# A decoder layer on one core: attention's queries, keys and values computed from high and low parts, their weights loaded a stage earlier

## The reference

```python
x = layernorm(x + mixer(x))        # layernorm, k, v, r = 256x256 projections, decayed cumulative sum, Wo
x = layernorm(x + xattn(x, ctx))   # this stage is changed
x = layernorm(x + ffn(x))          # dense expert + 32 routed experts, 4 per token, capacity 1280

def xattn(x, ctx):                 # 8 heads of 64
    q = x @ Wq                     # 256 -> 512
    k, v = ctx @ Wk, ctx @ Wv      # 192 -> 512
    attn = softmax(q k^T / 8)      # per batch and head, 128 x 128
    return (attn v) @ Wout + bout  # 512 -> 256
```

## Time and profile before

| what | us |
|---|---|
| median of three runs | 2421.14 |
| profiled execution | 2423.74 |
| its span, first to last instruction | 2422.2 |
| setup and mixer, about | 0 to 275 |
| attention with routing, about | 275 to 1131 |
| experts, about | 1140 to 2010 |
| combine, about | 2010 to 2422 |

### The profile page before, as it was taken

How to read it: one execution, slowest core, us unless ns; L and a number is a source line. 1 busy time by engine, 2 the same in 40 slices (tenths; PEclk the granted TensorE clock), 3 DMA queues, 4 the chain that set the end, 5 groups by cost and what they waited for, 6 DMA issues and landing times. The chain is left out here.

```text
span 2422.2 us, 51520 instructions
## 1 busy us (share of the span) xinstructions
PE 2123.5 (88%) x13848; PEld 1722.7 (71%) x13848; DVE 1574.4 (65%) x3953; ACT 1211.0 (50%) x3430; POOL 1351.9 (56%) x1648
## 2 busy tenths in 40 slices
PE   6999699999999999830999999999999956878884
PEld 3555356666666666530999999999999955777774
DVE  4666335667667666632777777777777743766666
ACT  2555245444455445410777777777777742222221
POOL 3666303456655655555555555555555535777775
PEclk9999899999999999955999999999999987989897
DMA  4000112322411321301666666666667643444343
GB/s 127 33 0 0 46 50 78 98 62 59 117 59 59 107 69 59 101 13 58 209 236 239 237 234 228 237 242 228 238 227 243 238 143 126 132 121 136 119 137 91
DMA packets 240146, 317.12 MB, mean 131 GB/s; under 512 B 38073, under 2 KB 161761, under 8 KB 240098
## 3 DMA queue, kind: packets, MB, share of 16 engines
q1 hardware_dynamic: 210594, 258.19, 31.9%
q0 software_dynamic: 29504, 58.37, 8.2%
HBM read 233.34 MB, written 83.14 MB: 131 GB/s over the span
## 5 line engine op out<-in xcount | busy, mean ns | idle before, releaser
L969 POOL DMA_INDIRECT slot_token<-tok,a_slot_i x256 | 267.9, 1047 | 231.0 <-issue 95.6
L1354 POOL DMA_INDIRECT e_xg<-x_rows,e_tok x188 | 197.4, 1050 | 346.2 <-DMA e_tok<-slot_token 188.1
L1639 POOL DMA_INDIRECT f_row<-expert_rows,f_idx x256 | 273.9, 1070 | 89.9 <-issue 76.7
L1532 DVE TENSOR_TENSOR e_hid<-e_sg,e_u 128x256 f32<-128x256 f32 x368 | 155.1, 421 | 133.3 <-PE e_u L1207 106.7
L1482 ACT ACTIVATE e_sg<-e_g 128x256 f32<-128x256 f32 x368 | 141.2, 384 | 179.6 <-PE e_g L1207 179.6
L852 ACT ACTIVATE a_prob<-a_s,a_ntop 128x128 f32<-128x128 f32 x512 | 180.2, 394 | 0.8 <-DVE a_ntop L1149 0.5
L1730 ACT ACTIVATE f_sg<-f_g 128x512 f32<-128x512 f32 x64 | 38.2, 597 | 222.1 <-PE f_g L1207 222.1
L1363 POOL TENSOR_TENSOR e_wd1l<-e_raw_d,e_wd1h 128x256 fp32r<-128x256 f32 x184 | 130.4, 742 | 30.0 <-ACT e_wd1h L1461 29.8
L1207 PE MATMUL f_d<-f_wdh,f_hth 128*128 128x256 f32 x256 | 85.6, 334 | 63.6 <-DVE f_htl L1759 63.6
L1363 POOL TENSOR_TENSOR e_wd0l<-e_raw_d,e_wd0h 128x256 fp32r<-128x256 f32 x184 | 130.9, 743 | 7.3 <-ACT e_wd0h L1461 6.4
L1207 PE MATMUL e_d<-e_wd1h,e_ht1h 128*128 128x256 f32 x368 | 108.3, 294 | 24.5 <-issue 24.5
(11 more groups left out here) (262 smaller groups left out, 7522.9 us busy)
## 6 DMA issues: line engine op xcount, KB each, us to landing
e_raw_g<-in_eg SPq DMA_DIRECT2D x94, 512.0 KB
e_raw_u<-in_eu SPq DMA_DIRECT2D x94, 512.0 KB, 4.2
e_raw_d<-in_ed SPq DMA_DIRECT2D x93, 512.0 KB, 5.0
expert_rows<-a_zero SPq DMA_DIRECT2D x16, 2560.0 KB, 11.8
expert_rows<-e_out SPq DMA_DIRECT2D x92, 256.0 KB, 2.2
x<-in_x SPq DMA_DIRECT2D x16, 512.0 KB, 3.4
x_rows<-x SPq DMA_DIRECT2D x16, 512.0 KB, 3.4
f_xs<-x_rows SPq DMA_DIRECT2D x16, 512.0 KB, 4.8
```

Of the source, the lines that this page charges most:

```text
L969: pool.indirect_dma_start(k.slot_tok, bass.IndirectOffsetOnAxis(ap=slot_i[:, j, q:q + 1], axis=0), k.tok[:, j:j + 1], None, bounds_check=S ...
L1354: pool.indirect_dma_start(xg[a][:, n, :], None, k.x2_d, bass.IndirectOffsetOnAxis(ap=tok[a][:, n:n + 1], axis=0))\
L1532: dve.tensor_tensor(hid[m % 2][:], sg[m % 2][:], bank_u[m % 2][:, 0:SETW], ALU.mult)\
L1639: pool.indirect_dma_start(row[a][:, j, q, :], None, k.out_d[0:SLOTS, :], bass.IndirectOffsetOnAxis(ap=idx[a][:, j, q:q + 1], axis=0))\
```

## The change

Each product of queries, keys and values is computed from parts. An operand is rounded to the type float32r (its high part, by a copy on ScalarE); the difference to the original, in float32r as well, is its low part. A product is high x high + high x low + low x high. Queries: two chunks of 128 rows, three passes each, six matmuls a job. Keys and values: the 192 context rows are one chunk of 128 (three passes) and one of 64. The last 64 rows are loaded twice, in the upper and the lower 64 partitions of one chunk; its upper half holds the high part, its lower half the low part, and the weights have their high part in both halves, so one pass gives high x high and high x low, and a fifth pass of 64 rows gives the weights' low part. The "t" jobs are emptied by both engines in turn: ScalarE writes the high part, VectorE the low part.

The context has one raw buffer and one split buffer instead of two. In slot 0, ScalarE rounds the next group's two chunks behind its exponentials, VectorE takes the low part of the stacked 64 rows behind the copy of the weighted values, and GpSimd takes the low part of the 128 rows between `rstd` and the scatters. SP waits for both parts before it loads the next group's context.

The weights and the first context are loaded by SP in the mixer, into buffers that later serve as the second buffers of queries, keys and values. At the head of the attention stage ScalarE and VectorE split them, and TensorE waits for the six low parts. The tables of the mixer are freed at its end to make room.

```diff
+def load_context(sp, k, dram, g):
+    cols = bass.ds(g * GW, GW)
+    sp.dma_start(k.ctx_raw[:, 0, :], dram["ctx"][0:P, cols]).then_inc(k.c_in, 16)
+    for side in range(2):
+        sp.dma_start(k.ctx_raw[side * DH:(side + 1) * DH, 1, :], dram["ctx"][P:CD, cols]).then_inc(k.c_in, 16)
# mixer, SP, behind the loads of x
+                sp.dma_start(k.turned["q"][:, 0:DC, :], dram["wq"].rearrange("(c p) n -> p c n", p=P)).then_inc(k.wp_in, 16)
+                load_context(sp, k, dram, 0)
+                for n in "kv":
+                    sp.dma_start(k.turned[n][:, 0, :], dram["wx" + n][0:P, :]).then_inc(k.wp_in, 16)
+                    for side in range(2):
+                        sp.dma_start(k.turned[n][side * DH:(side + 1) * DH, 1, :], dram["wx" + n][P:CD, :])\
+                          .then_inc(k.wp_in, 16)
+                sp.dma_start(k.wo[:], dram["wout"].rearrange("(c p) n -> p c n", p=P)).then_inc(k.wp_in, 16)
# attention
+        def with_context(weights, cols, tokens):
+            return [(weights[:, 0, cols], ct[:, 0, tokens]), (weights[:, 0, cols], ct[:, 1, tokens]),
+                    (weights[:, 1, cols], ct[:, 0, tokens]), (weights[:, 2, cols], ct[:, 2, tokens]),
+                    (weights[0:DH, 3, cols], ct[0:DH, 2, tokens])]
...
-                        for n in range(2):
-                            sp.wait_ge(a_done[n], ONE + before(g + 1, n))
+                        for split in (cl_rdy, cm_rdy):
+                            sp.wait_ge(split, ONE + g + 2)
                             apart(sp, k.past_sp)
-                        sp.dma_start(ct[par][:], ctx_d[:, :, bass.ds((g + 2) * GW, GW)]).then_inc(c_in[par], 16)
+                        load_context(sp, k, dram, g + 2)
...
-                            for c in range(DC):
-                                last = pe.matmul(out[:], wq[:, c, m * P:(m + 1) * P], xt[:, c, :],
-                                                 start=(c == 0), stop=(c == DC - 1))
+                            cols = slice(m * P, (m + 1) * P)
+                            last = split_product(pe, out[:], [((wq[0][:, c, cols], wq[1][:, c, cols]),
+                                                               (xt[0][:, c, :], xt[1][:, c, :])) for c in range(DC)])
...
-                pe.wait_ge(w_in, DMA + 48)
-                pe.wait_ge(wo_in, DMA + 16)
+                pe.wait_ge(k.wp_in, 8 * 16)
+                pe.wait_ge(wl_rdy, 6)
# ScalarE
+                def context_high(g):
+                    act.wait_ge(k.c_in, 48 * (g + 1))
+                    if not isinstance(g, int) or g:
+                        act.wait_ge(a_done[0], ONE + before(g - 1, 0) + upto(g - 1, "v", 2))
+                        act.wait_ge(a_done[1], ONE + before(g - 1, 1) + upto(g - 1, "v", 3))
+                    for c in range(2):
+                        act.activation(ct[:, 2 * c, :], k.ctx_raw[:, c, :], ACT.Copy).then_inc(ch_rdy, 1)
# GpSimd
+                def context_low(g):
+                    pool.wait_ge(ch_rdy, ONE + 2 * g + 1)
+                    pool.tensor_tensor(ct[:, 1, :], k.ctx_raw[:, 0, :], ct[:, 0, :].bitcast(F32), ALU.subtract)\
+                        .then_inc(cl_rdy, 1)
...
                         rstd(g - 1, not after and g == 1)
+                    if after or g + 1 < NG:
+                        context_low(g + 1)
# VectorE, emptied
+                        if kind == "t":
+                            dve.wait_ge(xh_rdy, ONE + DC * g + m + 1)
+                            dve.tensor_tensor(xt[1][:, m, :], bank_a[i][:], xt[0][:, m, :].bitcast(F32), ALU.subtract)\
+                               .then_inc(a_out[i], 1)
+                            continue
```

More of the change, by code:

```diff
@@ L546, in attention_stage @@
         p = Parts(nc, ctx, "a_")
[L547 to L553, removed]
+        wq = [p.sb(f"wq{h}", [P, DC, INNER], F32R) for h in "hl"]
+        wkv = {n: p.sb("w" + n, [P, 4, INNER], F32R) for n in "kv"}
+        wo = k.wo
+        xs = p.sb("xs", [P, TG, D])
+        xt = [p.sb(f"xt{h}", [P, DC, GW], F32R) for h in "hl"]
+        ct = p.sb("ct", [P, 3, GW], F32R)
+        qt, kt, vv = ([p.sb(n + "0", [P, IC, GW]), k.turned[t]] for n, t in (("qt", "q"), ("kt", "k"), ("vv", "v")))
         prob = [p.sb(f"prob{i}", [P, HEADS, T]) for i in range(2)]
@@ L586, in attention_stage @@
         bank_v, bank_o = p.bank("v"), p.bank("o")
-        w_in, wo_in = p.sem("w_in"), p.sem("wo_in")
-        c_in = [p.sem(f"c_in{i}") for i in range(2)]
+        wh_rdy, wl_rdy, ch_rdy, cl_rdy, cm_rdy, xh_rdy = (p.sem(n) for n in ("wh", "wl", "ch", "cl", "cm", "xh"))
         a_done, a_out = ([p.sem(f"{n}{i}") for i in range(2)] for n in ("a_done", "a_out"))
@@ L877, in slot @@
                         weights(s + 1, b + 1)
+                    if b == 0 and (not isinstance(g, int) or g + 1 < NG):
+                        context_high(g + 1)
                     emptied(g + 1, 1 - par, b, 1)
@@ L999, in _ @@
                 stage(0)
+                context_low(0)
                 for i in range(2):
@@ L1104, in place, with context_low, weights_low @@
                     assert then.done == STEPS, then.done
+                def context_low(g):
+                    dve.wait_ge(ch_rdy, ONE + 2 * g + 2)
+                    dve.tensor_tensor(ct[DH:P, 2, :], k.ctx_raw[DH:P, 1, :], ct[DH:P, 2, :].bitcast(F32), ALU.subtract)\
+                       .then_inc(cm_rdy, 1)
+                def weights_low():
+                    dve.wait_ge(wh_rdy, 1)
+                    dve.tensor_tensor(wq[1][:], k.turned["q"][:, 0:DC, :], wq[0][:].bitcast(F32), ALU.subtract)\
+                       .then_inc(wl_rdy, 2)
+                    for m, n in enumerate("kv"):
+                        for c, side in ((0, slice(0, P)), (1, slice(0, DH))):
+                            dve.wait_ge(wh_rdy, 2 + 2 * m + c)
+                            dve.tensor_tensor(wkv[n][side, 2 * c + 1, :], k.turned[n][side, c, :],
+                                              wkv[n][side, 2 * c, :].bitcast(F32), ALU.subtract).then_inc(wl_rdy, 1)
                 def emptied(g, par, b, f):
                     for kind, m, i in jobs(g, b, f):
+                        if kind == "t":
+                            dve.wait_ge(xh_rdy, ONE + DC * g + m + 1)
+                            dve.tensor_tensor(xt[1][:, m, :], bank_a[i][:], xt[0][:, m, :].bitcast(F32), ALU.subtract)\
+                               .then_inc(a_out[i], 1)
+                            continue
                         if i != 0:
@@ L1123, in emptied @@
                         else:
-                            out = {"t": xt, "k": kt[par], "v": vv[par], "rt": rxt}[kind]
+                            out = {"k": kt[par], "v": vv[par], "rt": rxt}[kind]
                             done = dve.tensor_copy(out[:, m, :], bank[:])
@@ L1179, in slot @@
                     dve.tensor_copy(ot[:], bank_v[:].rearrange("p (m t) -> p m t", m=IC)).then_inc(ot_rdy, 1)
+                    if b == 0 and (not isinstance(g, int) or g + 1 < NG):
+                        context_low(g + 1)
                     emptied(g + 1, 1 - par, b, 2)
+                weights_low()
+                context_low(0)
                 for b in range(TG):
```

67 lines of the change are left out of this document (43 added, 24 removed).

## The result

| kernel | median, us | runs | ratio |
|---|---|---|---|
| before | 2419.37 | 4 | |
| changed | 2381.78 (2380.92 to 2385.18) | 4 | 0.9848 [0.9835, 0.986] |

The change wins 1.5%. The sign was forecast, the size was not: 2381.78 lies above the range that ended at 2374. The profiled execution took 2382.58 us (span 2380.7).

What follows compares the result with a forecast made beforehand. TensorE was taken to bound the attention stage, with VectorE and GpSimd's loop close behind. Start and first fill 11.9, other groups 20.4, ten periods 40: 72.3 us, hence 2350, range 2340 to 2363 (8 in 10: 2328 to 2374).

Steps and rivals of the forecast that it cites:

- What bounds the kernel: Attention stage: TensorE near its limit, busy 45.01 of 46 us, with VectorE and GpSimd's loop some 2 us behind.
- The failed step: Key and value jobs: every pass, stacked or of 64 rows, priced at 0.232 us, so 1.16 us a job.
- The bound of 0.28 for any pass: Projection passes: upper price limit of 0.28 us each, 3.1 us more on the 64 passes of a group.
- I add 0.3, bounds 0 and 1.27: Slot 0: VectorE delayed 0.3 us by the port shared with GpSimd's new split, making the period 42.2 us.
- The start: Head of the attention stage: TensorE starts at 280.6 after the rounding, 6.0 us won, bounds 4.5 and 8.
- The first fill: From TensorE's start to the first scores: the 12 jobs of a group, 5.8 us won.
- GpSimd's loop, 42.3 us: Routing loop over GpSimd's scatters, token counter and VectorE's slot numbers: 42.3 us, or 41.1 if the landing wait absorbs the split.
- The groups at the ends: Groups outside the ten periods: 5.5, 4.7, 4.3 and 1.5 us won in the first four, 4.4 in the last.
- C: Rival: a lower clock for TensorE, the kernel slower or level; chance 0.04.
- D: Rival: the passes pay nothing on the path, only the start is won; period 46.1, 2410 us; chance 0.03.
- A: Rival: TensorE stays the bound, VectorE and GpSimd finding 2 us in overlaps; period 40.3 to 41.2, 2328 to 2340; chance 0.20.
- B: Rival: routing loop decides through late landings or a blocked port; period 43.5 to 45, 2363 to 2378; chance 0.17.

Runs made afterwards that it cites:

- full fifth pass: Changed kernel with its fifth key and value pass on all 128 rows instead of 64, adding low times low: 2369.54 us, ratio 0.979.
- later bias: Changed kernel with GpSimd's first addition of the bias waiting until the six low parts of the weights are made: 2380.65 us, ratio 0.9839.
- both context parts on VectorE: Changed kernel with a fifth pass of 128 rows, and VectorE making both context low parts in slot 0, GpSimd none: 2363.60 us, ratio 0.9764.
- alternate order: Changed kernel with every second key and value job running its five passes in reverse, the 64-row pass first: 2375.81 us, ratio 0.9813.
- the fills alone: Changed kernel, 64-row pass kept, with the 16 zero fills issued in the mixer instead of one per group: ratio 0.9867, on another chip.
- the seven kernels with the fills in the mixer: Seven kernels with the 16 zero fills issued in the mixer, not one a group in attention; with a fifth pass of 128 rows 2356.61 us.

## Why the prediction was wrong

- **What bounds the kernel: right.** TensorE decides in slots 1 and 2 and VectorE in slots 0 and 3, with a stall of 0.83 us before slot 0's transposes, less than the 1.5 to 2 forecast, and 0.54 before slot 1's.
- **The failed step: "The pass that stacks both halves of the last 64 rows, and the one of 64 rows, I price like the others, by the nearest row (0.232)."** The nearest row had no change of height in it. The stacked pass was priced well enough (ten full passes, two of them stacked and two in the place of the 64-row ones, take 2.58 us, 0.26 each with the slower first one, inside the bounds); the one of 64 rows cost about 0.53, 0.30 more than forecast. Six key and value jobs lie in slots 1 and 2: 6 x 0.3 = 1.8 of the 1.96 us missing there, and with a full fifth pass 1.7 of them came back (22.57 to 20.88 us). That is nearly all of the 2.0 us by which the period was missed, and so about 20 us of the time. The bound of 0.28 for any pass excluded it. In the trace of before the scores and the 96-row products change height as well, so the step could have been doubted.
- **"I add 0.3, bounds 0 and 1.27" for the port: the mechanism right, the size off.** The context part took 1.59 us instead of 0.6, and slot 0 came to 11.90 instead of 11.6. It was more than the 0.3 taken and inside the bounds.
- **The start: 3.1 instead of 6.0.** The bias and GpSimd's context part stretched VectorE's low parts. The run with the later bias restored 280.04, against 280.6 forecast. The collision that the prediction named for slot 0 was left out here. The first fill won 2.5 instead of 5.8: its eight key and value jobs each carry the pass of 64 rows (with a full one the fill takes 23.0 instead of 24.9 us, 284.11 to 307.11), TensorE waits 1.50 us for the low half of the rows (0.78 for one copy before), and 8.7 us of it ran at a granted clock of 0.50. Before, the stretch 286.56 to 296.00 had 0.64, which by the two levels is 6.8 us at the lower one.
- **GpSimd's loop, 42.3 us: right as a second bound, a little long, and it didn't decide.** The counter was written at T + 31.6 on the mean instead of 32.3, as only half of the split reached it; with the forecast's other terms that makes 41.6 us. The loop adds to the period where the jobs are shorter: with full passes the mean is 43.2 with the fills in the way and 42.6 without, and in the last two periods of either, in which VectorE doesn't wait for the counter, it is 42.3. Had the pass been priced rightly, the forecast for this kernel would have been close. Had the pass been free, the kernel would still have missed 2350, because the fills delay the landing (6.83 us against 3.50 in the same group, both context parts on VectorE; 6.18 against 2.42 with the alternate order): the full fifth pass, the nearest thing to the forecast's kernel, took 2369.54.
- **The groups at the ends: 12.2 instead of 21.8, and -1.2 instead of 4.4.** The first five periods, the fill in the first of them, won 2.3, 3.4, 3.0, 1.9 and 1.6 us, where 5.8, 5.5, 4.7, 4.3 and 1.5 were forecast; with a full fifth pass the first three won 2.1, 2.0 and 2.3 us more. The rest isn't traced. In the last group and behind it TensorE waits for GpSimd's counts and for the routed rows, and it did so before as well, so shorter jobs win nothing. From the last T to the same count product it is 103.1 us before and 103.3 now:

```profile
1065.88 0.77 PE L751 MATMUL a_a<-a_mask,before 128*128 128x128 f32 x2 [12.58 <-POOL count L951]
```
```profile
1031.34 0.76 PE L770 MATMUL a_a<-a_mask,before 128*128 128x128 f32 x2 [12.59 <-POOL count L1002]
```

- **Rivals.** C and D were rightly low, and A did not come: none of the ten periods was under 44. B named nearly the right time (2363 to 2378, missed by 4 us) and the right period (43.5 to 45) for a wrong reason in this kernel. It needed the counter at T + 33.5 or later in most groups; in the ten it came at T + 33.4 at the latest, VectorE waited in 3 of them, and the period did not move when the fills went.

## What to carry to other kernels

A pass is priced by the nearest row only if it also follows a pass of its own height. Count the changes of height, and give the array a full pass if that makes them go away, here by multiplying one more low part; it cost TensorE nothing, since a full pass takes the same 0.23 us. When a second bound lies close under the first, removing the first is worth little until both are treated: the full pass alone gave 12 us, the fills alone nothing on the periods, together 25. A new GpSimd pass of two SBUF inputs is to be drawn on the same line as VectorE's own, at the start of a stage as in the loop: VectorE's differences cost 2.3 times their own length in the loop and 3.5 times at the start.

## What the hardware showed that I had not expected

- A visit to a 64-row pass amid 128-row ones: 0.30 us over a pass of full height, 0.42 for two side by side.
- VectorE's 64x512 difference: 0.69 us alone, 1.59 beside GpSimd's 128x512. Two of 128x512: 1.27 alone, 4.50 beside GpSimd's bias and difference.
- The first split pass after other work takes 0.30 to 0.34 us, the next ones 0.23.
- The landing of a group's scatters, without zero fills, goes more by the group than by the kernel: in the seven kernels with the fills in the mixer GpSimd's first wait was 4.0 to 4.7 us, its second 2.1 to 2.7, its ninth 3.7 to 4.2, and the later ones nearly all 1.33. With fills in flight the waits were 1.3 to 7.3. What makes the early groups slower is open.
- The start's lower clock after 16.26 us without work: a granted 0.50, at which a pass takes 0.43 us.
